# Attention with routed experts: the attention loop re-cut so that each pass holds one batch's scores, the tail of the one before and the start of the next

## The reference

```python
xn = _layernorm(x)
# attention: 16 heads of 16, rotary embedding, causal
q, k, v = xn @ Wq.T, xn @ Wk.T, xn @ Wv.T
q, k = _rope(q, k)
attn = softmax(where(causal, -inf, q k^T / sqrt(16)))
a = (attn v) @ Wo.T
# experts: 4 of 32, hidden size 128, and a shared one of 512
topk_scores, topk_idx = top_k(softmax(xn @ router_w.T + router_bias), 4)
topk_scores = topk_scores / sum(topk_scores)
f = sum_j topk_scores_j * expert_j(xn) + silu(xn @ sgate_w.T) * (xn @ sup_w.T) @ sdown_w.T
out = x + a + f
```

## Time and profile before

| | us |
|---|---|
| median of 3 runs | 2676.68 (2672.46 to 2676.88) |
| profiled execution | 2683.8 |
| its span | 2681.6 |
| start, to the first scores | 41.8 |
| batch 0 | 118.8 |
| batches 1 to 14 (loop) | 1615.3 |
| batch 15 | 157.9 |
| experts and summing | 745.6 |

### The profile page before, as it was taken

One profiled execution on the slowest core, in us unless ns is written; L12 is line 12 of the kernel. 1 busy time (PEld: TensorE's weight loads), 2 busy tenths in 40 slices (PEclk: granted clock), 3 DMA queues, 4 the chain that ended last, 5 costly groups with the idle time before them and its releaser, 6 DMA issues. The chain is left out here.

```text
span 2681.6 us, 43680 instructions
## 1 busy us (share of the span) xinstructions
PE 1982.5 (74%) x11279; PEld 1203.6 (45%) x11280; DVE 1349.7 (50%) x3123; ACT 871.7 (33%) x1668; POOL 997.4 (37%) x993
## 2 busy tenths in 40 slices
PE   5778888778788778888777888861888888887700
PEld 2344443334444333443434444330477777776600
DVE  5645546364564545546454454630344444444467
ACT  1323233132322313223232323310255556555500
POOL 4523333432333433233442333446044444444500
PEclk8878888877887877888887887885799999999955
DMA  6052250505325051441505235052544444444389
GB/s 154 25 91 44 60 89 17 100 17 86 51 53 89 22 95 28 75 60 43 98 20 87 43 60 89 22 93 94 175 135 136 136 135 144 138 138 134 101 295 331
DMA packets 217833, 254.99 MB, mean 95 GB/s; under 512 B 74549, under 2 KB 166462, under 8 KB 217664
## 3 DMA queue, kind: packets, MB, share of 16 engines
q1 hardware_dynamic: 160128, 161.90, 28.9%
q0 software_dynamic: 35840, 71.63, 7.8%
q10 hardware_dynamic: 21824, 20.98, 2.5%
HBM read 112.54 MB, written 94.64 MB: 77 GB/s over the span
## 5 line engine op out<-in xcount | busy, mean ns | idle before, releaser
L715 DVE TENSOR_REDUCE neg<-ps_u 128x2 f32<-128x768 f32 (+3 forms) x384 | 392.7, 1044 | 365.9 <-PE ps_u L935 175.5
L494 POOL DMA_INDIRECT table<-entry,slot x256 | 253.8, 991 | 560.9 <-ACT xs L578 462.1
L1207 POOL DMA_INDIRECT y_dram<-yb_all,ent x288 | 283.5, 984 | 327.2 <-ACT yb_all L1163 233.0
L962 PE MATMUL ps_u<-q_st,k_st 50*128 50x512 f32 (+3 forms) x1024 | 205.1, 463 | 188.1 <-DMA q_st<-neg_t 107.4
L915 PE MATMUL ps_g<-we_gu 128*128 128x512 f32 x512 | 263.7, 647 | 60.1 <-DVE hid L702 43.9
L496 POOL DMA_INDIRECT values<-xs,slot x256 | 248.8, 972 | 83.3 <-issue 83.3
L600 ACT ACTIVATE we_d<-ps_u 128x1024 f32<-128x1024 f32 x160 | 163.5, 1023 | 345.0 <-PE ps_u L973 149.7
L931 PE MATMUL ps_u<-k_st,q_st 48*128 48x128 f32 (+3 forms) x1024 | 196.3, 421 | 74.7 <-DVE neg L715 26.2
L481 POOL TENSOR_TENSOR we_d<-we_d 128x512 f32<-128x512 f32 x64 | 81.3, 1270 | 440.8 <-DVE we_d L685 438.0
L962 PEld LDWEIGHTS ps_u<-q_st,k_st 50*128 50x128 f32 x1024 | 106.5, 239 | 290.0 <-issue 113.0
L600 ACT ACTIVATE probs<-ps_u 128x1024 f32<-128x1024 f32 x160 | 161.5, 1022 | 196.2 <-PE ps_u L973 167.4
(11 more groups left out here) (155 smaller groups left out, 3005.6 us busy)
## 6 DMA issues: line engine op xcount, KB each, us to landing
xg<-values SPq DMA_DIRECT2D x288, 128.0 KB
ys<-y_dram SPq DMA_DIRECT2D x64, 512.0 KB, 5.4
q_st<-we_gu SPq DMA_DIRECT2D x192, 128.0 KB
k_st<-we_gu SPq DMA_DIRECT2D x192, 128.0 KB
we_gu<-x SPq DMA_DIRECT2D x16, 512.0 KB
xres<-x SPq DMA_DIRECT2D x16, 512.0 KB
sum_dram<-osum SPq DMA_DIRECT2D x16, 512.0 KB
we_gu<-wgu_e ACTq DMA_DIRECT2D x16, 512.0 KB
```

What stands on the lines that cost most here:

```text
L494: pool.indirect_dma_start(table[:, :], bass.IndirectOffsetOnAxis(ap=slot[:, k:k + 1], axis=0), entry[:, k, :], None).then_inc(scattered, 16)
L715: nc.vector.tensor_reduce(neg[:, g % 2, i, :, k0:k0 + nk], ps[:, :, 0:nk * n].rearrange("p a (k n) -> p a k n", n=n), AX.X, ALU.max, negat ...
L962: nc.tensor.matmul(ps[:, a, lo:lo + n], k_st[rows, h, kt * P:(kt + 1) * P], q_st[rows, h, kt * P:SEQ], start=(lo == 0), stop=False, skip_g ...
L1207: pool.indirect_dma_start(y_dram[:, :], bass.IndirectOffsetOnAxis(ap=ent[k][:, 0:1], axis=0), yb[k][:, :], None, bounds_check=TOKENS * TOP ...
```

## The change

`ORDER` is cut into four sections with one pattern: section g holds `s1` of group g+1, `av` of group g-1 and `s2` of group g. So `s1` of group 0 belongs to the next batch, and `av` of group 3 and the output products (now one step `out`, in four parts) to the batch before. These steps move over the border of the pass; `ahead_of` says by how much. The gate and up products read a copy `xn_g` of the normalized input, which ScalarE makes at the end of a pass (`xng`), so that `xn_t` can be overwritten earlier. `route` has three parts. The input load moves from SyncE's queue to ScalarE's (`xload`), and the load and the store at the output get steps of their own (`xres`, `store`). Two links of the chain `back` get own semaphores. `LAST_ORDER` is written out for the last batch: the scatters and the fill at its head, the weight loads two at a time from `s2` of group 2 on. An `EPILOGUE` does group 3's `av` and the output of the last batch. Cut to its core:

```diff
 ORDER = [
-    ("rankC",), ("gate", 0), ("placeV",), ("s1", 0, 0), ("gth", 0), ("up", 0), ("s1", 0, 1), ("copy",), ("s1", 0, 2),
...
-    ("av", 3, 3), ("avT", 3), ("rankB",), ("down", 2), ("down", 3), ("oproj", 0), ("oproj", 1),
+    ("rankC",), ("xload",), ("copy",), ("scat", 0), ("s1", 1, 0),
+    ("av", 3, 0), ("av", 3, 1), ("av", 3, 2), ("av", 3, 3), ("s1", 1, 1), ("avT", 3), ("gate", 0), ("placeV",), ("scat", 1),
...
+    ("rankB",), ("s2", 3, 2), ("qk", 3), ("s1", 0, 5), ("s2", 3, 3), ("negsplit", 0), ("part0", 3), ("xng",), ("s2", 3, 4),
+    ("negT", 0), ("stack", 1),
 ]
...
+EPILOGUE = [
+    ("av", 3, 0), ("av", 3, 1), ("av", 3, 2), ("av", 3, 3), ("avT", 3), ("out", 0, 0), ("out", 0, 1), ("out", 1, 0),
+    ("out", 1, 1), ("store",),
+]
...
-        if step[0] == "s2" and step[1:] != (0, 0) and piece < GU_PIECES:
-            s.append(("load_gu", piece))
-            piece += 1
+        if step[0] == "s2" and step[1] >= 2:
+            n = 2 if piece < 12 else 1
+            s += [("load_gu", piece + k) for k in range(n)]
+            piece += n
...
+def ahead_of(step):
+
+    if step[0] in NEXT_STEPS or (step[0] in ("s1", "negsplit", "negT") and step[1] == 0):
+        return 1
+    if step[0] in ("out", "store") or (step[0] in ("av", "avT") and step[1] == NG - 1):
+        return -1
+    return 0
...
-            lb, lu = steps(FIRST_STEPS, 0, 0, True, [None] * 3, [None] * 2)
-            lb, lu = steps(body, 0, 1, False, one_later(lb), lu)
-            lb, lu = one_later(lb), one_later(lu)
+            lb, lu = steps(FIRST_STEPS, 0, True, [None] * 3, [None] * 2)
+            lb, lu = steps(ORDER, 0, False, lb, lu, left_out=-1)
             with eng.Fori(1, BATCH - 1) as b:
-                assert (lb, lu) == tuple(map(one_later, steps(body, b, b + 1, False, lb, lu)))
-            steps(tail, BATCH - 1, None, False, lb, lu)
+                assert (lb, lu) == steps(ORDER, b, False, lb, lu)
+            lb, lu = steps(tail, BATCH - 1, False, lb, lu)
+            steps(EPILOGUE, BATCH, False, lb, lu)
...
-                    act.wait_ge(pe["up"], NM * nb)
+                    act.wait_ge(pe["qk"], NCH * nb)
+                    act.wait_ge(xg_ready, nb)
...
+            def x_load(nb, step, env):
+
+                act.wait_ge(xn_ready, NT * nb)
+                act.dma_start(xin[:, :, :], x[bass.ds(nb * SEQ, SEQ), :].rearrange("(t p) d -> p t d", p=P)
+                              ).then_inc(x_in, 16)
+
+            def for_gate(nb, step, env):
+
+                act.wait_ge(pe["up"], NM * nb)
+                for c in range(KC):
+                    ins = nc.scalar.activation(xn_g[:, c, :], xn_t[:, c, :], ACT.Copy)
+                ins.then_inc(xg_ready, 1)
...
-                back.link(b, nc.vector.tensor_copy(np_[:, :, 0, :], n_))
+                nc.vector.tensor_copy(np_[:, :, 0, :], n_).then_inc(neg_high, 1)
+                dve.wait_ge(neg_high, NG * b + g + 1)
...
-                back.link(b, nc.vector.reciprocal(rden[:], rows[:, :, DH]))
+                nc.vector.reciprocal(rden[:], rows[:, :, DH]).then_inc(rden_ready, 1)
+                dve.wait_ge(rden_ready, NG * b + g + 1)
...
+                    if k == 0 and m == 0:
+                        pe_.wait_ge(xg_ready, b + 1)
...
-                        ins = nc.tensor.matmul(ps[:, :], w_gu[:, c, lo:lo + P], xn_t[:, c, :], start=(c == 0),
+                        ins = nc.tensor.matmul(ps[:, :], w_gu[:, c, lo:lo + P], xn_g[:, c, :], start=(c == 0),
                                                stop=(c == KC - 1))
...
+            def out_part(b, step, env):
+
+                p_, half = step[1:]
+                t = 2 * p_ + half
+                if half == 0:
+                    bank_of(step, 0, env)
+                ps = ps_g[env[0][("out", p_, 0), 0][0]][:, half * D:(half + 1) * D]
                 if t == 0:
-                    unit_of(step, env)
                     pe_.wait_ge(S["hidden"], done("hidden", b, NM - 1))
```

More of the change, by code:

```diff
@@ new lines @@
+    ("negsplit", 3), ("gth", 2), ("exps",), ("up", 2), ("s2", 2, 4), ("negT", 3), ("part0", 2),
[3 rows of a table added]
+    ("negT", 0), ("stack", 1),
+]
+LAST_ORDER = [
+    ("rankC",), ("fill_rows",), ("copy",), ("scat", 0), ("scat", 1), ("scat", 2), ("scat", 3), ("fill",), ("s1", 1, 0),
[3 rows of a table added]
+    ("out", 1, 1), ("s2", 0, 4), ("up", 0), ("negT", 1), ("store",), ("xres",),
[6 rows of a table added]
+    ("negsplit", 3), ("s2", 2, 4), ("negT", 3),
+    ("av", 2, 0), ("av", 2, 1), ("av", 2, 2), ("av", 2, 3), ("avT", 2), ("s2", 3, 0), ("s2", 3, 1), ("s2", 3, 2),
+    ("s2", 3, 3), ("s2", 3, 4),
+]
@@ L248, in phase_a @@
         xn_t = in_gu([P, KC, SEQ])
+        xn_g = in_gu([P, KC, SEQ])
         rp1 = in_d([P, 2, SEQ])
```

180 lines of the change are left out of this document (88 added, 92 removed), and 29 rows, old and new, of tables (LAST_ORDER, ORDER).

## The result

The changed kernel takes **2755.3 us** (2746.5 to 2762.0, 4 runs) against 2676.8 (2672.5 to 2677.6, 4 runs): a ratio of 1.0295, 95% interval 1.0264 to 1.0326. It is 2.9% slower; I had forecast 2548 us. The profiled execution's span is 2744.6 us, 63.0 more than before.

The account below looks back on a forecast made before the run. TensorE was taken as the bound, with idle stretches and a low clock on top. Loop -113, start -11 and last batch -5 gave -129 us: span 2681.6 to 2552.6, as a median 2548 us; range 2410 to 2655.

Parts of the forecast that it names:

- First `s2` of a group: In each loop batch, TensorE's wait on the store of the neg rows before `s2` disappears: -6.9 us a batch.
- Bursts: GpSimd's two runs of 16 indirect DMAs a batch stay unchanged; TensorE has output products in hand during the first: -1.7 us.
- stacks: The 24 copies to `q_st` and `k_st`, each half now beside a run of GpSimd's DMAs: taken as 0 us.
- the late part: From 9 to 12 us after a GpSimd burst's start to 2 us past its end; TensorE's signals 5 to 11 us late.
- Clock: In the loop, fewer TensorE idle stretches win back some of the 18 busy us at 1.2 GHz: -2 us a batch.
- Added holds: Two new ScalarE copies a batch and `part0` at group ends, holding ScalarE's queue: +2.5 us a batch, bounds 0 and 6.
- Start: Start and first batch, which loses `av` of a previous group and output products but gains batch 1's group 0: -11 us.
- Last batch: The batch after the loop, with its unchanged burst of 64 DMAs, falls from 157.9 to 153 us: -5 us.
- Sum of a batch: All per-batch terms of the loop together: -8.1 us, so 107.3 us a batch in place of 115.4.
- Rival A: Stack copies worsen GpSimd's bursts, signals late from their start through a backlog of scatter transfers: 2855 us, chance 0.13.
- B: TensorE's idle time in the bursts only moves, 8 to 11 us whatever stands there: 2646 us, chance 0.15.
- C: Output products and spaced gate and up steps keep TensorE at work in the bursts, clock up: 2390 us, chance 0.17.

## Why the prediction was wrong

*First `s2` of a group, -6.9.* Right as far as it went: no wait on the neg rows is left. But it bought nothing, for TensorE now stands at other `s2` and score steps inside the burst, on signals that are late.

*Bursts, -1.7, and stacks, 0.* **This is the step that failed.** I let each burst run beside 12 stack copies and kept the late part where I had read it, from 9 to 12 us on and 5 to 11 us late. That reading was too mild already: the loop before has late units from 6.0 us on, and the one of the earlier trace rows, read at 304.59, had ended at 292.18, 12.4 us before. I also didn't look at TensorE's own work at the burst's start: the first burst now begins in the middle of 32 attention-value matmuls, where it had none near it; the second stands right behind such a block as it did before. It measured: late signals for units that end from 2.2 us on in the first burst and from 5.3 in the second, within bursts 6.5 us late in the mean in place of 2.1, and TensorE's idle time up by 7.7 us a batch where the forecast had it fall. Copies and small matmuls were each seen to make signals later in the kernel before, at a cost of at most 2 us a batch there; bursts moved off both gained 7% in the changed kernel. How the two share it in the new order, and why it costs more there, wasn't separated.

*Clock, -2.* TensorE's busy time fell by 3.0 us a batch, at a granted clock of 0.83 against 0.82. The size was about right and the reason wrong: there is more idle time, not less. What lowered the busy time wasn't tested.

*Added holds, +2.5.* By the kernels without scatters the whole new order costs +0.8 a batch, this included. *Start, -11:* measured -5. *Last batch, -5:* measured +17. TensorE stands there for 3.2, 28.2, 5.0, 10.1 and 21.2 us in this order, 67.7 in all, since after each release it soon waits for the next reader.

*Sum of a batch:* -8.1 forecast, +4.8 measured. *Rival A* had the symptom, late signals near the burst's start, and its sign (within the first 5 us, it said; 2.4, and 5.3 in the second burst). The cause that it names, a backlog of the scatters' own transfers, wasn't tested. I gave it 0.13 because the late part stood at one place in both bursts of the kernel before; but neither of these had copies beside it, so it was no evidence on copies. Its price was too high, +11.9 us a batch for the +4.8 measured. *B*'s mark, idle time above 21 us a batch, is there too, but not its time; *C* is out.

The length of a DMA on GpSimd stayed at 0.97 us in the new bursts; the rule of the Trainium skill that I had weighed (SBUF — State Buffer, 🔬 SBUF: two separate sides) played no part. Over all 512 scatters a DMA took 0.98 us in the mean and at most 1.24 before, 0.97 and at most 1.40 after, so none grew as I had worked out from the rule. Which of VectorE's operations hold the port no row tells, so the rule itself wasn't tested.

**Left open:** what holds TensorE's signals back, why two of the five chips don't do it, and what the pause after every 113th scatter is. The plain changed kernel ran on none of these two; its four-burst version is 1.5% slower there.

## What to carry to other kernels

When one engine's signals come late beside another's burst, what stands in the burst is part of the price: before moving copies or dense small matmuls there, try the cheap edits, a shorter run or a shift by a few us. Cutting the two bursts of 16 into four of 8 gave the kernel before 8% here, more than the reordering had promised. And run the baseline beside every variant: by the chip it took 2677 or 2084 us, and while pauses gave the changed kernel 9% on one kind of chip, three other kernels with pauses were 7 to 10% slower than the kernel before on the other.

## What the runs showed of the hardware

- Outside GpSimd's runs of indirect DMAs, a reader on VectorE or ScalarE that stood idle at a score unit's end started 0.04 to 0.09 us after it in the mean. Inside them, on three chips, units of the loop were read up to 17.3 us after their end (the second profile of the plain changed kernel). On two chips, in eight traces, no such idle reader started more than 0.13 us after.
- Answers to TensorE aren't late: in the two kernels' loops each wait of TensorE of over 1 us in a burst ended at most 0.15 us after the last instruction that it can have waited for.
- The lateness needs scatters on end: on those three chips runs of 16 in 20.1 us make it, runs of 8 make less in the kernel before (1.0 us in the mean for 2.3), and a pause of 2.4 us after every 4 leaves 0.6 us in the changed kernel.
- In every trace GpSimd pauses for 3.0 to 9.9 us after each 113th indirect DMA of the loop.
- More idle time needn't cost time: with 3.0 us more of it a batch, beside the copies, TensorE's busy time was 3.3 less at a granted clock of 0.83 against 0.81, on another chip of the same kind.
